# Attention scores from one fp32r product over 96 stacked rows, in an attention and expert kernel on one core

## The chip, the cores and the metric

The kernel runs on one core of a Trainium2 chip. The metric is the device time of one execution in microseconds (us), smaller is better. The core's engines are named as the profile names them: PE (TensorE) and its weight loads PEld, DVE (VectorE), ACT (ScalarE), POOL (GpSimd) and SP (SyncE, which here only issues DMAs).

## The reference, cut to what matters

Two layers run one after the other over x (8 batches x 256 tokens x 256). The change touches only the first mixing step of layer 0, which has 8 heads of 32 dimensions, so 64 pairs of batch and head. q is the layer norm of x, and k and v are both the context:

```python
gate_in = concat([q, k, v], -1)
ig = (gate_in @ igate_w.T + igate_b).T ; fg = (gate_in @ fgate_w.T + fgate_b).T
log_f_cum = cumsum(log_sigmoid(fg))
log_D = where(lower_triangle, log_f_cum[s] - log_f_cum[t] + ig[t], -inf)
max_log_D = max(log_D, over t)
D = exp(log_D - max_log_D)
C = (qh @ kh.T / sqrt(32)) * D
normalizer = maximum(abs(sum(C)), exp(-max_log_D))
h = (C / (normalizer + 1e-6)) @ vh
h_norm = (h - mean(h)) / sqrt(var(h) + 1e-5) * norm_w      # per head
```

After it come a 32-expert layer (top 4), a long convolution with two small feed-forward blocks, and a dense mixture of 8 experts. None of their instructions is changed.

## The kernel before, in words

Semaphores are written by hand, and each engine runs its own list in order.

**Front.** PE transposes the context (L1726, `mix_turned`), two batches and one half of the 256 features at a time, into a PSUM bank, and ACT copies each bank to kT (`mix_copy`, L1215): eight banks. Then PE computes the gates' share of k (`gates`, L1732, started by a wait for all eight copies), and after that the same for q: xn (the normalised rows, DVE L515) is transposed, copied to qT by ACT, and multiplied by the gate weights. `gates_done` releases a chain of small row operations on ACT and DVE (rg, r1, rF, rM, AE, MHL, L520 to L533), which ends with `rows_done`, a transpose by PE (L1759), and aT and eE (L1234, L1235). MHL holds for each of the 64 pairs the negated maximum in two fp32r parts, the high part in rows 0 to 63 and the low part in rows 64 to 127. `sel` (DVE L504) is a table of 64 stationary matrices that pick one pair's two rows out of MHL. `spare` (L1719) issues products whose result nobody reads.

**Scores.** In the loop over i, the 64 pairs, PE runs `scores(i)` and then `values(i - 2)`. `scores` multiplies kT by a masked copy of q in full fp32 over 128 rows, of which 96 are zero: POOL copies the 32 rows of one head into a zeroed slot of qM (`mask_queries`, L1583, 12 slots). The 384 score columns of a head are 256 for the first half of the keys and 128 for the second. Each fp32 product shows as two MATMUL records. The second half of `scores` forms the exponent's argument in another bank: the mask in bf16 over 384 columns (L1777) and the selected maxima in two products of 256 and 128 columns (L1778, L1779).

**Per pair.** ACT exponentiates in two pieces (L1271, L1272), DVE multiplies scores by decay (`mixed`, L603), and PE multiplies the result by v extended by a column of ones (L1788 to L1790, 33 columns each, three products of two passes). Score banks, argument banks and Dm are double, Cm is triple: `scores(i)` waits until DVE has mixed pair i - 2.

**Per batch.** For each finished group of eight pairs DVE does `head_work` in four parts, spread over the next group's pairs: part 0 the normaliser (L562 to L567), part 1 the scaled heads hN (L577), part 2 the mean (L581, L582), and part 3, after ACT has squared (`square`, L1244), the variance (L586, L587). POOL subtracts the mean (`centre`, L1607) and finishes (`finish`, L1596 to L1600: a power, two multiplications, an addition into x). The last two batches are finished by DVE after the loop.

**SP's queue** is in order: loads of ident, context, x and bcv; sixteen stores of zeros into slots_in (L416, 768 KB each); the six convolution constants (L421, after gates_done and vext_done); and, after the last pair's values, gi and w0.

What sets the order around the change is this list:

```python
for i in range(B * NH):          # PE
    scores(i)
    if i >= 2:
        values(i - 2)
```

Of the kernel before, what the change touches and what calls it, by code (L numbers as in the profile page):

```python
# [4 lines left out]
F32 = mybir.dt.float32  # L5
# [8 lines left out]
P = 128  # L14
# [6 lines left out]
NF = 192  # L21
FLOW = 64
# [3 lines left out]
EPS = 1e-5  # L26
ARENA = 212800 // 64 * 64
# [23 lines left out]
def build(nc, dram, out_d):  # L51
    ctx = ExitStack()
    with ctx:
# [70 lines left out]
        vext = at("vext", [P, NT, NH, DH + 1])  # L124
        maskT = at("maskT", [P, 384], BF16)
        idb = at("idb", [P, P], BF16)
        gwt = at("gwt", [P, 6, 16])
# [3 lines left out]
        den = at("den", [P, 2, NH])  # L131
# [10 lines left out]
        sel = at("sel", [P, 64, P], F32R, start["dcw"])  # L142
# [4 lines left out]
        qM = at("qM", [P, 12, SEQ], F32, start["wS"])  # L147
# [3 lines left out]
        Cm = at("Cm", [P, 3, 384], F32, end["Dm"])  # L151
        rg = at("rg", [P, 256], F32, start["sc0"])
# [7 lines left out]
        MHL = at("MHL", [P, 256], F32R, end["ones"])  # L160
        id2 = at("id2", [P, 64], F32, end["MHL"])
# [56 lines left out]
        hN = at("hN", [P, 2, 512], F32, start["h1T"])  # L218
        hQ = at("hQ", [P, 2, 512], F32, end["hN"])
# [7 lines left out]
        assert end["Cm"] <= start["tF"] and end["kc"] <= end["tF"] and end["h1T"] <= start["Dm"] and end["id2"] <= end["cw2"]  # L227
        assert end["hC"] <= end["xn"] and end["hQ"] <= start["Dm"] and end["GI"] <= end["vext"] and end["WF"] <= end["eS"]
# [24 lines left out]
        sel_done = sem("sel_done")  # L253
# [12 lines left out]
        q_masked = sem("q_masked")  # L266
# [6 lines left out]
        head_scaled = sem("head_scaled")  # L273
        head_centred = sem("head_centred")
# [3 lines left out]
        last_centred = sem("last_centred")  # L278
# [47 lines left out]
        residual_added = sem("residual_added")  # L326
        xs_d = nc.dram_tensor("slots_in", (TILES * P, D), F32, kind="Internal").ap()
# [55 lines left out]

        def f32(ap):
            return ap.bitcast(F32)
# [13 lines left out]
        def _(sp):  # L399
# [12 lines left out]

            sp.wait_ge(zero_done, 1)
# [4 lines left out]
            sp.wait_ge(gates_done, 1)  # L418
            sp.wait_ge(vext_done, 1)
            for t, n in ((FZ, "fz"), (FW, "fw"), (Win, "win"), (peT, "pet"), (Wp1, "wp1"), (Wp2, "wp2")):  # L420
                sp.dma_start(t[tuple(slice(None) for _ in t.shape)], dram[n]).then_inc(conv_loaded, 16)  # L421
# [28 lines left out]
        def _(dve):  # L450
# [52 lines left out]
            dve.wait_ge(id2_done, 1)  # L503
            dve.tensor_copy(sel[:, :, :], id2[:, :].unsqueeze(2).to_broadcast([P, 64, P])).then_inc(sel_done, 1)  # L504
# [11 lines left out]
            dve.wait_ge(ctx_loaded, 16)  # L516
            dve.tensor_copy(vext[:, :, :, 0:DH], cx[:, :, :].rearrange("p n (h d) -> p n h d", h=NH)).then_inc(vext_done, 1)
# [41 lines left out]
            def head_normaliser(b, o):  # L559

                dve.wait_ge(pv_done, 8 * (b + 1))
                dve.tensor_copy(den[:, :, :], o[:, :, :, DH])  # L562
                link(dve.tensor_tensor(ut[:, 0, :, :], o[:, :, :, DH], constant(4, [P, 2, NH]), ALU.mult))
# [5 lines left out]
            def head_work(b, part):  # L569
# [3 lines left out]
                if part == 0:  # L573
                    head_normaliser(b, o)
# [24 lines left out]
            for i in range(B * NH):  # L599
# [1728 lines left out]
```

## Time and profile before

| | |
|---|---|
| Median of three runs | 1803.17 us (1802.14 to 1806.01) |
| Span of the profiled execution, first to last instruction | 1787.3 us |
| PE busy in the span | 1667.1 us, 93% |
| DVE, ACT, POOL busy | 1207.9 us, 474.6 us, 471.5 us |
| Mean granted TensorE clock | 0.971 of full speed |
| Front, from the start to the first score product | 46.5 us |
| Loop over 64 pairs | 110.9 us |

The page gives the profiled execution by its span. The median of the runs is 15.9 us above it; this lies before the first and behind the last recorded instruction, or is the difference of one run from another. A matmul's recorded duration includes its way through a pipelined array, so durations of neighbours overlap; how much PE time one takes is read from the distance between two starts. In rows of the timeline the first column is the start in us, the second the duration, and "xN" the merged records.

### The profile page before, as it was taken

The page shows a single profiled execution, that of the slowest core. Times are in us where ns is not written, and L with a number is a line of the kernel's source. Part 1 is how long each engine was busy: PE and PEld are TensorE (multiplying, and loading weights), DVE is VectorE, ACT ScalarE, POOL GpSimd, SP SyncE. Part 2 cuts the span into 40 slices and gives each one's busy share as a digit, 9 for nine tenths or more (in the row PEclk, how much of TensorE's full clock was granted, in tenths as well). Part 3 has the DMA queues.
Part 4 walks back from the last instruction along what each step waited for, and adds up shares of the span by engine and source line. Part 5 has one row for each costly group of instructions (what it writes and reads, how often), then busy time and mean ns, then how long its engine had stood idle before and what let it go on. Part 6 is the DMA issues. An engine that isn't in the chain of part 4 may idle for free.

```text
span 1787.3 us, 29133 instructions
## 1 busy us (share of the span) xinstructions
PE 1667.1 (93%) x9784; PEld 1439.4 (81%) x9785; DVE 1207.9 (68%) x2483; ACT 474.6 (27%) x836; POOL 471.5 (26%) x355
## 2 busy tenths in 40 slices
PE   6998987799956898999999999999999999999998
PEld 5997673388854787888888888888888888888887
DVE  6457777556656895666666766766766766766765
ACT  3445322134432464211211211211111111111111
POOL 4274257688426601100100100100100100100100
PEclk9998999899978998999999999999999999999999
DMA  9200022278643200000000000000000000000001
GB/s 368 91 1 30 16 73 96 89 250 272 200 127 119 72 1 19 19 36 18 19 34 18 20 33 18 21 32 18 21 32 18 23 30 18 26 27 18 18 0 48
DMA packets 53827, 106.53 MB, mean 60 GB/s; under 512 B 6528, under 2 KB 37696, under 8 KB 53632
## 3 DMA queue, kind: packets, MB, share of 16 engines
q1 hardware_dynamic: 19920, 63.33, 10.4%
q10 hardware_dynamic: 27696, 25.51, 4.5%
q0 software_dynamic: 6144, 16.79, 2.9%
q8 instruction: 43, 0.70, 0.2%
q14 instruction: 24, 0.20, 0.0%
HBM read 69.96 MB, written 35.65 MB: 59 GB/s over the span
## 4 chain that ended last, share of the span: by engine, by line
PE 80%; DVE 6%; issue 4%; POOL 4%; DMA 4%; ACT 2%; SPq 0%; POOLq 0%; DVEq 0%; another core or an unknown queue 0%; ACTq 0%
PE ps L1921 39%; PE ps L1937 20%; PE ps L2028 4%; DMA slots_in<-xn,idS 2%; POOL slots_in L1648 2%; PE ps L2047 2%; PE ps L1772 2%; PE ps L2103 1%; PE ps L2125 1%; PE ps L2008 1%; DVE x L917 1%; DMA x<-in_x 1%; PE ps L1773 1%; PE ps L1789 1%; PE ps L1790 1%
## 5 line engine op out<-in xcount | busy, mean ns | idle before, releaser
L1921 PE MATMUL ps<-xTH,wH 128*128 128x512 f32 x1024 | 402.5, 393 | 2.1 <-DVE hF L1161 2.1
L1921 PE MATMUL ps<-xTH,wL 128*128 128x512 f32 x1024 | 402.2, 393 | 0.0
L1921 PE MATMUL ps<-xTL,wH 128*128 128x512 f32 x1024 | 398.9, 390 | 0.0
L1309 ACT ACTIVATE sg<-ps 128x512 f32<-128x512 f32 x264 | 157.9, 599 | 885.3 <-PE ps L1921 885.3
L1161 DVE TENSOR_TENSOR hF<-sg,ps 128x512 f32<-128x512 f32 x256 | 175.7, 686 | 302.1 <-ACT sg L1309 302.1
L1620 POOL TENSOR_TENSOR wL<-wS,wH 128x1536 fp32r<-128x1536 f32 x32 | 111.9, 3496 | 959.8 <-ACT wH L1304 959.8
L1937 PE MATMUL ps<-wL,hH 128*128 128x256 f32 x1024 | 289.8, 283 | 0.0
L1937 PE MATMUL ps<-wH,hL 128*128 128x256 f32 x1024 | 289.7, 283 | 0.0
L1937 PE MATMUL ps<-wH,hH 128*128 128x256 f32 x1024 | 288.6, 282 | 0.5 <-DVE hL L1170 0.5
L1170 DVE TENSOR_TENSOR hL<-hF,hH 128x512 fp32r<-128x512 f32 x256 | 258.0, 1008 | 0.1
L1921 PEld LDWEIGHTS ps<-xTL,wH 128*128 128x128 f32 x1024 | 192.8, 188 | 42.2
L1180 DVE SCALAR_TENSOR_TENSOR x<-ps,cw,x 128x256 f32<-128x256 f32 x512 | 222.6, 476 | 1.0 <-PE ps L1937 1.0
L1921 PEld LDWEIGHTS ps<-xTH,wH 128*128 128x128 f32 x1024 | 193.6, 189 | 36.1 <-ACT sg L1309 1.9
L1921 PEld LDWEIGHTS ps<-xTH,wL 128*128 128x128 f32 x1024 | 193.8, 189 | 30.5
L1937 PEld LDWEIGHTS ps<-wH,hH 128*128 128x128 f32 x1024 | 195.5, 191 | 10.6 <-DVE hL L1170 0.7
L1937 PEld LDWEIGHTS ps<-wH,hL 128*128 128x128 f32 x1024 | 195.5, 191 | 9.8
L1937 PEld LDWEIGHTS ps<-wL,hH 128*128 128x128 f32 x1024 | 195.5, 191 | 0.0
L1164 DVE CAST hH<-hF 128x512 fp32r<-128x512 f32 x256 | 109.3, 427 | 38.8 <-PE ps L1937 30.2
L1648 POOL DMA_INDIRECT slots_in<-xn,idS x64 | 76.6, 1197 | 59.6 <-DMA slots_in<-xn,idS 29.7
L2028 PE MATMUL ps<-eHL,hH 128*128 x384 | 81.5, 295 | 2.2 <-POOL eHL L1635 2.2
L1687 POOL DMA_INDIRECT yg<-slots_out,idG x48 | 50.0, 1041 | 69.2 <-DMA slots_out<-yo 49.0
L603 DVE SCALAR_TENSOR_TENSOR Cm<-ps,Dm 128x384 f32<-128x384 f32 x64 | 35.6, 557 | 47.1 <-ACT Dm L1272 43.0
(385 smaller groups left out, 2525.4 us busy)
## 6 DMA issues: line engine op xcount, KB each, us to landing
wS<-in_w SPq DMA_DIRECT2D x32, 768.0 KB, 4.3
slots_in<-eS SPq DMA_DIRECT2D x16, 768.0 KB, 20.2
eS<-in_wr SPq DMA_DIRECT2D x32, 384.0 KB, 3.9
xl<-slots_in ACTq DMA_DIRECT2D x48, 256.0 KB, 3.9
slots_out<-yo ACTq DMA_DIRECT2D x48, 256.0 KB, 3.1
cx<-in_ctx SPq DMA_DIRECT2D x1, 2048.0 KB, 10.4
x<-in_x SPq DMA_DIRECT2D x2, 1024.0 KB, 13.8
out<-x SPq DMA_DIRECT2D x4, 512.0 KB, 2.9
```

The source lines that it names most:

```text
L1161: dve.tensor_tensor(hF[:, b, :], sg[:, b, :], ps[:, 2 + b, :], ALU.mult).then_inc(mul_done, 1)
L1164: dve.tensor_copy(hH[:, b, :], hF[:, b, :]).then_inc(h_high, 1)
L1170: dve.tensor_tensor(hL[:, b, :], hF[:, b, :], f32(hH[:, b, :]), ALU.subtract).then_inc(h_low, 1)
L1180: dve.scalar_tensor_tensor(x[:, tile, :], acc, cw2[:, tile, bass.ds(it, 1)], x[:, tile, :], ALU.mult, ALU.add).then_inc(evac_done, 1)
L1309: act.activation(sg[:, b, :], ps[:, b, :], ACT.Silu).then_inc(silu_done, 1)
L1620: pool.tensor_tensor(blocks(wL, slot, plain), blocks(wS, slot, plain), f32(blocks(wH, slot, plain)), ALU.subtract).then_inc(w_low, 1)
L1648: pool.indirect_dma_start(xs_d, bass.IndirectOffsetOnAxis(ap=idS[:, n, k:k + 1], axis=0), xn[:, n, :], None, bounds_check=TILES * P - 1, o ...
L1687: pool.indirect_dma_start(slot_rows(n)[:, k, :], None, ys_d, bass.IndirectOffsetOnAxis(ap=idG[:, n, k:k + 1], axis=0), bounds_check=TILES ...
L1772: pe.matmul(ps[:, i % 2, 0:256], kT[:, c, t0:t0 + P], qM[:, i % 12, :], start=True, stop=True)
L1921: last = pe.matmul(ps[:, 2 * half + b, :], piece(w, s, slot, col, P), v[:, k, g * 512:(g + 1) * 512], start=q == 0, stop=q == 5)
L1937: last = pe.matmul(o, h[:, b, t * P:(t + 1) * P], piece(w, s, slot, col, D), start=(opens and t % 2 == 0 and q == 0), stop=(closes and q = ...
L2028: last = pe.matmul(ps[:, 2 + b, t * D:(t + 1) * D], h[:, b, (2 * t + k) * P:(2 * t + k + 1) * P], eFlat[:, bass.ds(off + (w + k * D), D)], ...
```

## The change

The scores come from one fp32r product over 96 rows instead of a full fp32 one over 128. k and q are split into a high part (fp32r) and a low part. `parts` holds them in the transposed layout. They are stored to memory, and for each group of four heads loaded back so that 96 partitions hold, for k, the rows high, low, high, and for q the rows high, high, low of one head (`load_stack`). One product over those 96 rows gives the three leading terms. Four stacks are in the kernel at a time, sixteen are used.

- ACT copies each transposed k bank twice, once as fp32r high part and once as kT. DVE makes the high parts of q. POOL makes all low parts (16 subtractions of 128x512). The masked copies of q, qM and their memset go.
- SP stores the parts (16 DMAs, 8.4 MB in all), loads the stacks (96 DMAs of 128 KB, 12.6 MB), and issues the zero stores between the later stack loads, one per stack.
- The 128-column piece comes first in the banks, so the mask product covers 256 columns and the selector is one product over 384 columns; MHL gains a copy of its second half. The selector is a column of id2 read with step 0; `sel` and its 7.70 us cast go.
- v gets a second extra column, the mean of v over the head, so the mean comes out of the values product (34 columns). `head_work` has three parts; `centre` goes; the normaliser is no longer divided out but enters the variance as eps times its square.
- The constants FZ to Wp2 are issued before the zero stores, not after.

```diff
+            def store_parts(to, g, signal):
+                for i in range(2):
+                    sp.dma_start(to[i, :, :, g * 512:(g + 1) * 512], f32(parts[:, i, :, g * 512:(g + 1) * 512])).then_inc(signal, 16)
+            def load_stack(j):
+                b, c = j // 2, j % 2
+                if j >= STACKS:
+                    sp.wait_ge(qk_done, 4 * (j - STACKS + 1))
+                sp.wait_ge(k_stored[b // 2], 32)
+                sp.wait_ge(q_stored[b // 2], 32)
+                for a, (of, order) in enumerate(((kp_d, (0, 1, 0)), (qp_d, (0, 0, 1)))):
+                    for r, i in enumerate(order):
+                        src = of[i, :, c, b * SEQ:(b + 1) * SEQ].rearrange("(h d) t -> d h t", d=DH)
+                        sp.dma_start(f32(stack(j)[r * DH:(r + 1) * DH, a, :, :]), src).then_inc(stack_loaded[j % STACKS], 16)
+            for g in range(4):
+                sp.wait_ge(k_low, 2 * g + 2)
+                store_parts(kp_d, g, k_stored[g])
+            for g in range(4):
+                sp.wait_ge(q_low, 2 * g + 2)
+                store_parts(qp_d, g, q_stored[g])
+                if g == 0:
+                    load_stack(0)
+            sp.wait_ge(gates_done, 1)
+            for j in range(1, STACKS):
+                load_stack(j)
...
             for a in range(TILES * D // UW):
+                if STACKS + a < 2 * B:
+                    load_stack(STACKS + a)
                 sp.dma_start(zv[a], eS[:, 0:2, :].rearrange("p i c -> p (i c)")).then_inc(zeros_stored, 16)
...
-            dve.wait_ge(id2_done, 1)
-            dve.tensor_copy(sel[:, :, :], id2[:, :].unsqueeze(2).to_broadcast([P, 64, P])).then_inc(sel_done, 1)
...
+            for g in range(4):
+                last = dve.tensor_reduce(vext[:, 4 * g:4 * g + 4, :, DH + 1], vext[:, 4 * g:4 * g + 4, :, 0:DH], AXX, ALU.add)
+                if g == 3:
+                    link(last)
+                    dve.tensor_scalar(vext[:, :, :, DH + 1], vext[:, :, :, DH + 1], 1.0 / DH, None, ALU.mult).then_inc(vext_done, 1)
+                dve.wait_ge(k_stored[g], 32)
+                for c in range(2):
+                    cols_ = slice(g * 512, (g + 1) * 512)
+                    dve.wait_ge(mixT_copied, 8 + 2 * g + c + 1)
+                    dve.tensor_copy(parts[:, 0, c, cols_], qT[:, c, cols_]).then_inc(q_high, 1)
...
-            link(dve.tensor_copy(MHL[0:64, :], r1[0:64, :]))
-            link(dve.tensor_tensor(r2[0:64, :], r1[0:64, :], f32(MHL[0:64, :]), ALU.subtract))
-            dve.tensor_copy(MHL[64:, :], r2[0:64, :]).then_inc(rows_done, 1)
+            link(dve.tensor_copy(MHL[0:64, P:], r1[0:64, :]))
+            link(dve.tensor_tensor(r2[0:64, :], r1[0:64, :], f32(MHL[0:64, P:]), ALU.subtract))
+            dve.tensor_copy(MHL[0:64, 0:P], r1[0:64, P:])
+            dve.tensor_copy(MHL[64:, 0:P], r2[0:64, P:])
+            dve.tensor_copy(MHL[64:, P:], r2[0:64, :]).then_inc(rows_done, 1)
...
                 if part == 0:
-                    head_normaliser(b, o)
+                    dve.wait_ge(pv_done, 8 * (b + 1))
+                    link(dve.tensor_copy(den2[:, :, :, :], o[:, :, :, DH:DH + 2]))
+                    dve.tensor_tensor(hC[:, b, :].rearrange("p (s h d) -> p s h d", s=2, h=NH), o[:, :, :, 0:DH],
+                                      den2[:, :, :, 1].unsqueeze(3).to_broadcast([P, 2, NH, DH]), ALU.subtract).then_inc(head_read, 1)
                 if part == 1:
+                    link(dve.scalar_tensor_tensor(den, den, -1.0, den, ALU.mult, ALU.max))
+                    link(dve.tensor_tensor(den, den, eE[:, :, 8 * b:8 * b + 8], ALU.max))
+                    link(dve.tensor_scalar(den, den, 1e-6, DEN_MAX, ALU.add, ALU.min))
+                    link(dve.scalar_tensor_tensor(mean[:, b % 2, :, :], den, EPS, den, ALU.mult, ALU.mult))
...
-                if i >= 8 and i % 8 in (2, 3, 4):
+                if i >= 8 and i % 8 in (2, 3):
                     head_work(b - 1, i % 8 - 2)
                 if i >= 16 and i % 8 == 1:
-                    head_work(b - 2, 3)
+                    head_work(b - 2, 2)
...
             for j in range(8):
+                act.wait_ge(mixT_done, j + 1)
+                act.activation(parts[:, 0, j % 2, (j // 2) * 512:(j // 2 + 1) * 512], ps[:, j % 4, :], ACT.Identity)
                 mix_copy(j, kT[:, j % 2, (j // 2) * 512:(j // 2 + 1) * 512])
...
-            link(pool.memset(qM[:, :, :], 0.0))
+                    pool.tensor_tensor(parts[:, 1, c, cols_], src[:, c, cols_], f32(parts[:, 0, c, cols_]), ALU.subtract).then_inc(signal, 1)
+            low_parts(kT, 0, k_low)
+            low_parts(qT, 8, q_low)
...
             def scores(i):
-                pe.wait_ge(q_masked, i + 1)
-                pe.matmul(ps[:, i % 2, 0:256], kT[:, c, t0:t0 + P], qM[:, i % 12, :], start=True, stop=True)
-                pe.matmul(ps[:, i % 2, 256:384], kT[:, c, t0 + P:t0 + SEQ], qM[:, i % 12, P:],
-                          start=True, stop=True).then_inc(qk_done, 1)
+                j = i // 4
+                k, q = (stack(j)[0:3 * DH, a, i % 4, :] for a in range(2))
+                wait(pe, mixed_done, i - 1)
+                if i % 4 == 0:
+                    pe.wait_ge(stack_loaded[j % STACKS], 96 * (j // STACKS + 1))
+                pe.matmul(ps[:, i % 2, P:384], k[:, 0:P], q, start=True, stop=True)
+                pe.matmul(ps[:, i % 2, 0:P], k[:, P:], q[:, P:], start=True, stop=True).then_inc(qk_done, 1)
                 wait(pe, decay_done, i - 1)
-                pe.matmul(ps[:, 2 + i % 2, 0:384], idb[:, :], maskT[:, :], start=True, stop=False, skip_group_check=True)
-                pe.matmul(ps[:, 2 + i % 2, 0:256], sel[:, i, :], MHL[:, :], start=False, stop=False, skip_group_check=True)
-                pe.matmul(ps[:, 2 + i % 2, 256:384], sel[:, i, :], MHL[:, P:SEQ], start=False, stop=True,
+                pe.matmul(ps[:, 2 + i % 2, 0:256], idb[:, :], maskT[:, 0:256], start=True, stop=False, skip_group_check=True)
+                pe.matmul(ps[:, 2 + i % 2, 0:384], id2[:, i:i + 1].to_broadcast([P, P]), MHL[:, :], start=False, stop=True,
                           skip_group_check=True).then_inc(arg_done, 1)
```

## Rows read from the trace of the kernel before

**Rows 1.** Busy time by stretch: span part, busy us and records per engine, clock, DMA
```profile
0.00:46.50 46.50, 31.77 (x176) 25.68 (x177) 31.19 (x87) 15.12 (x27) 20.09 (x39) 1.00 0.99 370
46.50:157.40 110.90, 110.20 (x833) 105.87 (x833) 62.27 (x162) 50.53 (x135) 64.47 (x81) 1.00 0.09 31
```

**Rows 2.** Waits from 46 to 157 us: total us, times, longest
```profile
ACT Dm L1271 <- PE ps L1779: 59.1, 64, 1.6
DVE Cm L603 <- ACT Dm L1272: 43.0, 50, 1.5
```

**Rows 3.** Timeline, one pair of the loop, from score product to score product
```profile
80.18 0.68 PE L1772 MATMUL ps<-qM,kT 128*128 128x256 f32 x2
...
80.69 0.38 PE L1773 MATMUL ps<-qM,kT 128*128 128x128 f32 x2
...
80.91 0.33 PE L1777 MATMUL ps<-maskT,idb 128*128 128x384 bf16 x1
...
81.25 0.36 PE L1788 MATMUL ps<-vext,Cm 128*128 128x33 f32 x2
...
81.45 0.47 ACT L1271 ACTIVATE Dm<-ps,aT 128x256 f32<-128x256 f32 x1 [0.98 <-PE ps L1779]
...
81.83 0.36 ACT L1272 ACTIVATE Dm<-ps,aT 128x128 f32<-128x128 f32 x1
...
81.89 0.68 PE L1772 MATMUL ps<-qM,kT 128*128 128x256 f32 x2
...
82.27 0.56 DVE L603 SCALAR_TENSOR_TENSOR Cm<-ps,Dm 128x384 f32<-128x384 f32 x1 [0.45 <-issue]
```

**Rows 4.** Timeline, PE in the last stage, fp32r products of 256 and 512 columns
```profile
800.18 0.28 PE L1937 MATMUL ps<-wL,hH 128*128 128x256 f32 x1
800.30 0.40 PE L1921 MATMUL ps<-xTH,wH 128*128 128x512 f32 x1
800.53 0.40 PE L1921 MATMUL ps<-xTH,wL 128*128 128x512 f32 x1
```

**Rows 5.** Timeline, DVE in the loop, a mix and the head work behind it
```profile
65.14 0.56 DVE L603 SCALAR_TENSOR_TENSOR Cm<-ps,Dm 128x384 f32<-128x384 f32 x1 [1.16 <-ACT Dm L1272]
65.61 0.17 DVE L562 COPY den<-ps 128x16 f32<-128x16 f32 x1
...
66.10 0.17 DVE L565 TENSOR_TENSOR den<-den,eE 128x16 f32<-128x16 f32 x1
66.31 0.18 DVE L566 TENSOR_TENSOR den<-den,kc 128x16 f32<-128x16 f32 x1
...
67.44 0.68 DVE L577 TENSOR_TENSOR hN<-ps,den 128x512 f32<-128x512 f32 x1
```

**Rows 6.** Timeline, the front: copies of k, its gates, the last row cast
```profile
12.90 0.60 ACT L1215 ACTIVATE kT<-ps 128x512 f32<-128x512 f32 x1 [4.13 <-PE ps L1726]
...
16.31 2.07 ACT L1215 ACTIVATE kT<-ps 128x512 f32<-128x512 f32 x4 [0.25 <-PE ps L1726]
...
18.52 7.15 PE L1732 MATMUL ps<-kT,gateW 128*128 128x256 f32 x32 [0.88 <-ACT kT L1215]
...
44.99 0.29 DVE L533 CAST MHL<-r 64x256 fp32r<-64x256 f32 x1
```

**Rows 7.** Timeline, POOL and DVE just after the loop
```profile
157.55 1.26 POOL L1599 TENSOR_TENSOR hC<-hC,bcv 128x512 f32<-128x512 f32 x1
157.74 1.10 DVE L564 TENSOR_TENSOR den<-den,ut 128x16 f32<-128x16 f32 x1
```

**Rows 8.** Timeline, SP's DMA issues
```profile
11.86 19.25 SPq L416 DMA_DIRECT2D slots_in<-eS  x16
...
37.59 0.46 SPq L421 DMA_DIRECT2D FW<-in_fw  x1
```

**Rows 9.** Busy time by stretch, columns as in rows 1, around the loop's end
```profile
155.00:158.00 3.00, 2.84 (x22) 2.44 (x21) 1.99 (x6) 0.73 (x2) 2.84 (x3) 1.00 0.00 0
158.00:161.00 3.00, 3.00 (x7) 0.62 (x5) 2.86 (x5) 0.00 (x0) 2.10 (x2) 0.77 0.86 314
```

More of the change, by code:

```diff
@@ L21 @@
 NF = 192
+STACKS = 4
 FLOW = 64
@@ L26 @@
 EPS = 1e-5
+DEN_MAX = 1e15
 ARENA = 212800 // 64 * 64
@@ L140, in build @@
         assert top[0] - base <= ARENA, top[0] - base
-        sel = at("sel", [P, 64, P], F32R, start["dcw"])
+        parts = at("parts", [P, 2, 2, NT * P], F32R, start["dcw"])
+        stackA = at("stackA", [P, 2, 2, 4, SEQ], F32R, start["wS"])
+        stackB = at("stackB", [P, 2, 2, 4, SEQ], F32R, start["xTH"])
         qT = at("qT", [P, 2, NT * P], F32, start["xTH"])
@@ L151, in build @@
         Cm = at("Cm", [P, 3, 384], F32, end["Dm"])
+        gwt = at("gwt", [P, 6, 16], F32, start["Cm"])
         rg = at("rg", [P, 256], F32, start["sc0"])
@@ L159, in build @@
         ones = at("ones", [P, 256], F32, end["AE"])
-        MHL = at("MHL", [P, 256], F32R, end["ones"])
-        id2 = at("id2", [P, 64], F32, end["MHL"])
+        MHL = at("MHL", [P, 384], F32R, end["ones"])
+        id2 = at("id2", [P, 64], F32R, end["MHL"])
         hC = at("hC", [P, B, 512], F32, start["xn"])
@@ L217, in build @@
         wf = at("wf", [P, 4, D], F32, start["vext"])
-        hN = at("hN", [P, 2, 512], F32, start["h1T"])
-        hQ = at("hQ", [P, 2, 512], F32, end["hN"])
+        hQ = at("hQ", [P, 2, 512], F32, start["h1T"] + 4096)
         WF = at("WF", [P, 8, D], F32, start["eS"])
@@ L227, in build @@
         assert end["Cm"] <= start["tF"] and end["kc"] <= end["tF"] and end["h1T"] <= start["Dm"] and end["id2"] <= end["cw2"]
+        assert end["parts"] <= end["ya"] and end["stackA"] <= start["FW"] and end["stackB"] <= end["xTH"]
         assert end["hC"] <= end["xn"] and end["hQ"] <= start["Dm"] and end["GI"] <= end["vext"] and end["WF"] <= end["eS"]
@@ L265, in build @@
         rowsT_copied = sem("rowsT_copied")
-        q_masked = sem("q_masked")
+        k_low = sem("k_low")
+        q_high = sem("q_high")
+        q_low = sem("q_low")
+        k_stored = [sem(f"k{g}_stored") for g in range(4)]
+        q_stored = [sem(f"q{g}_stored") for g in range(4)]
+        stack_loaded = [sem(f"stack{i}_loaded") for i in range(STACKS)]
         qk_done = sem("qk_done")
@@ L382, in pairs_done, with stack @@
             return 0 if isinstance(k, int) and k <= 0 else k * 2 + 1
+        def stack(j):
+            return (stackA, stackB)[j % STACKS // 2][:, j % 2, :, :, :]
         def f32(ap):
@@ L410, in load @@
                 sp.dma_start(blocks(wS, slot, plain), src.rearrange("p (a c) -> p a c", c=BLK)).then_inc(stage_loaded[slot], 16)
+            def store_parts(to, g, signal):
[22 more added lines that the diff above has]
+                load_stack(j)
+            sp.wait_ge(vext_done, 1)
+            for t, n in ((FZ, "fz"), (FW, "fw"), (Win, "win"), (peT, "pet"), (Wp1, "wp1"), (Wp2, "wp2")):
+                sp.dma_start(t[tuple(slice(None) for _ in t.shape)], dram[n]).then_inc(conv_loaded, 16)
             sp.wait_ge(zero_done, 1)
@@ L1238, in square @@
             def square(b):
-                if b < B - 1:
-                    act.wait_ge(head_centred, b + 1)
-                else:
-                    act.wait_ge(last_centred, 1)
+                act.wait_ge(head_read, b + 1)
                 wait(act, head_var, b - 1)
@@ L2262, in constants @@
     mask = np.zeros((P, 3 * P))
-    mask[:, 0:P] = mask[:, 2 * P:] = np.where(t <= s, 0.0, -1e30)
+    mask[:, 0:P] = mask[:, P:2 * P] = np.where(t <= s, 0.0, -1e30)
     tri = np.stack([(t < s) * 1.0, np.ones((P, P))], 1)
```

99 lines of the change are left out of this document (27 added, 72 removed).

## The prediction

> **What bounds the kernel now.** I read the busy time by stretch first, because the change touches two stretches only. The front lasts 46.5 us and the loop over 64 pairs 110.9 us [rows 1]; everything behind keeps its instructions. In the loop PE is busy for 110.20 of 110.90 us at full granted clock, DVE and ACT for about half. The waits agree: ACT waits for PE's argument product before each of the 64 pairs, 59.1 us in all, and DVE waits for ACT, 43.0 us [rows 2]. So PE paces the loop, and what counts is the distance between its starts.
>
> One pair's row of starts [rows 3]: score products 80.18 and 80.69, mask 80.91, values 81.25, next pair 81.89. So a pair costs 1.71 us: 0.51 + 0.22 for the scores, 0.34 for mask and selectors (384 + 256 + 128 columns), 0.64 for values. 64 x 1.71 = 109.6, and 1.3 us of start and end make up the 110.9.
>
> **The change, part by part.**
>
> *Scores.* Two fp32r products of 256 and 128 columns. An fp32r product of 256 columns takes 0.12 us to the next start, one of 512 takes 0.23 [rows 4], so time goes with columns. I take 0.12 for the first. The second is not in the trace in this form: half of it is 0.06, and a values product's six passes in 0.64 [rows 3] say that about 0.11 goes to each new stationary block, however few columns follow. I take 0.09, bounds 0.06 and 0.12. That 96 rows are used instead of 128 I cost at nothing. Saved: 0.73 - 0.21 = 0.52 a pair.
>
> *Mask and selector.* 640 columns instead of 768: 0.34 x 640/768 = 0.28, saves 0.06. *Values* with 34 columns instead of 33: 0.64 as before. PE's pair becomes 0.12 + 0.09 + 0.28 + 0.64 = 1.13 us.
>
> *Does something else bind at 1.13?* The chain over two pairs: `scores(i)` waits for the mix of pair i - 2. Today from the first score product to ACT's start is 1.27 us, from there to DVE's mix 0.82, the mix 0.56 [rows 3]; with 0.04 for PE's restart and 0.58 less in front the ring is 0.69 + 0.82 + 0.56 + 0.04 = 2.11 for two pairs, 1.06 each. That is only 0.07 below PE. Today's slack of 0.37 a pair is gone, so what DVE does between mixes now shows.
>
> *DVE's head work.* A mix holds DVE for 0.47 until the next operation starts; a small linked operation costs 0.21, one over 512 elements 0.68 [rows 5]. The new part 0 is a copy and a subtraction, 0.91; part 1 four small ones, 0.84; part 2 a reduction and a small one, 0.93. Each sits behind the mix of pair 2, 3 or 1 of eight, so these three take 3 x 0.47 + 2.68 = 4.09 us against PE's 3.39: 0.70 late in eight pairs, and with nearly no slack PE doesn't win it back. ACT's square (0.5) lands on two exponentials of 0.38 each [rows 3]: 1.26 against 1.13, 0.15 late. Eight pairs: 9.04 + 0.85 = 9.9, or 1.24 a pair. Loop: 64 x 1.24 + 1.3 = 80.7, **30.2 us less**. Bounds: PE alone, 64 x 1.13 + 1.3 = 73.6 (37.3 less); head work costing its whole 2.68 + 0.5 in each eight, 0.12 for the short product and some port waits, about 1.45 a pair and 94 (17 less).
>
> *Feeding the stacks.* PE's only new wait is for `stack_loaded` before each fourth pair; all PE work queues behind it. An issue on SP costs 0.46 (FW [rows 8]). Stack 0 is stored and loaded once the first q parts exist, around 34 us; stacks 1 to 3 follow gates_done, 18 issues of 0.46, 8.3 us from about 42, before pair 4 is due. In the loop four pairs (5.0 us) need seven issues, 3.2 us, and 1.57 MB (a stack and a zero store); at the 370 GB/s of the front [rows 1] that is 4.2 us, asked for 12 pairs ahead. So the loop's transfers are hidden, by 0.8 us in 5. The zero stores are read long after the loop; their old 19.25 us of issue [rows 8] overlapped the front. The six constants are issued ahead of them, needed only at 157. All at nothing.
>
> *The front.* ACT now copies each k bank twice. Four copies take 2.07, 0.52 each; the first starts at 12.90 and the last ended at 18.38, and PE's gates of k started at 18.52 on that release [rows 6]. Sixteen copies end at 12.9 + 16 x 0.52 = 21.2: 2.8 us later. Behind `gates(kT)` are PE's transposes of q, its gates and so gates_done, in order, so the 2.8 passes through to rows_done. Two more casts of half length before rows_done, against 0.29 for a full one [rows 6]: +0.5. The `sel` cast ran while DVE waited for x: nothing back. DVE's four reductions of v and eight casts of q, and POOL's subtractions, lie beside PE's work on q: the same number of gate products as for k, 7.15 [rows 6], and the transposes, some 10 us together.
>
> *A port.* A 16-column DVE operation on SBUF takes 0.17 alone [rows 5] but 1.10 when a POOL subtraction or product over 512 is under way, and ends with it [rows 7]. The front gets 16 such POOL operations beside DVE's small root steps and q casts. I take 0.5 for the delay, bounds 0 and 2 (two stalls of 1.1). The Trainium skill, "SBUF — State Buffer", on the shared port pair, says that a DVE instruction with two SBUF inputs and a GpSimd one that reads SBUF exclude each other for the whole instruction. By that rule POOL's eight q subtractions and DVE's eight q casts would run strictly in turn, 8 x 1.26 and 8 x 0.4, 13 us (an estimate) beside PE's 10, and the sum would be some 2 us higher, 1779; the trace agrees on the small operation, and nothing in it shows a cast being held.
>
> Front: 2.8 + 0.5 + 0.5 = **3.8 us more**, bounds 2.8 and 6. A gain I see only in x arriving with fewer stores beside it, some tenths.
>
> *Behind the loop.* DVE loses a reduction and a subtraction, but PE goes on with products of its own until ACT is freed, so 0.
>
> **Sum.** -30.2 + 3.8 = -26.4. It is made against the profiled span of 1787.3 us: 1760.9. The median lies 15.9 above the span, and I keep that distance: 1803.2 - 26.4 = **1776.8 us**.
>
> **The rivals.**
>
> 1. *The clock falls in the loop (slower).* At 158 to 161 us the granted clock drops from 1.00 to 0.77 as a mean, which is its two levels 2.4 and 1.2 GHz mixed, although PE's records look full; ahead of it PE ran the last values products, short ones, at 155 to 158 [rows 9]. The new loop has a larger share of those: 0.64 of 1.24 us instead of 0.64 of 1.71, with gaps. At 1.2 GHz a pair would cost 2 x 1.13 = 2.26, the whole loop 146, and the sum +35.1 + 3.8: 1842. It decides from (26.4 / (2.26 - 1.24)) = 26 pairs at the low level on; with fewer it only eats the gain, near 1792 with 15. Against it: the loop before holds 1.00 throughout, its last three us included [rows 1, 9]. The Trainium skill, "TensorE: Matmul & The Clock Gate", Part 1, says that the throttled state is the default and activity releases it; taken alone it would allow this case and gives no reason to rule it out. 0.06 for the full case, 0.08 for the partial one.
>
> 2. *The stacks arrive late.* The rows have 1 KB runs and three partition groups of 32; the trace shows no such transfer. At 250 GB/s instead of 370, 1.57 MB take 6.3 us, 1.57 a pair for the last 48 pairs: 48 x 0.33 = 16 more, 1793. For it: the cover is 0.8 us in 5. Against: twelve pairs of lead. 0.08.
>
> 3. *The score product doesn't get cheaper,* because an fp32r product on stacked rows runs at the pace of the full fp32 one. Then a pair stays at 1.65, the loop at 107, and the gain of 4 is what the front costs: 1803. Rows 4 speak against it. 0.04.
>
> **How the numbers follow.** The forecast, loop at 1.13 to 1.4 a pair, has 0.72, the rivals 0.26, and 0.02 stays for a front that costs over 25 us. Within the forecast the low end is 1803.2 - 37.3 + 2.8 = 1768.7 and the high one 1803.2 - 17 + 6 = 1792. A DVE whose part lateness is absorbed, with x early, could give 3 us more, so I set 1766; the top goes to 1794 to hold the late stacks. Outside are the two slow cases, rival 3 and part of rival 1. About 0.2%, 3.6 us, is what a measurement of this kernel can tell from no change. Faster: 0.72 + 0.08 + 0.08 = 0.88; same 0.04; slower 0.08.
>
> **What the profile would show.** Right: the distance between a pair's first score starts at 1.13 in the pairs without head work and over 1.3 in pairs 1 to 3 of eight; the score products 0.12 and 0.09 apart; DVE above 70% busy in the loop; `gates(kT)` starting at about 21.3 and the loop at about 50.3; no wait of PE on DMA in the loop; clock 1.00 in it. Wrong: PE waiting for the stack loads, a clock under 1.00 inside the loop, SP's issues nearer 1 us than 0.46, or the loop starting after 53.

## The result, and the profile after

The changed kernel takes 1849.15 us (median of four runs, 1842.77 to 1854.84) against 1804.59 for the kernel before beside it (1802.14 to 1809.28): 1.0242 times as long, interval 1.0207 to 1.0278, 44.6 us more. It is slower, where 26 us less was forecast. Executions of one kernel can differ in where the clock falls: where some held it and some did not, the experiments below list the times, or give the ratio of those that held it and name the other.

The page's clock line of the changed kernel, one digit for each fortieth of the span:

```profile
PEclk9555699879996799899999999999999999999999
```

Between about 46 and 185 us the granted clock is near half. Busy time by stretch (span part, busy us and records of PE, PEld, DVE, ACT, POOL, clock, DMA share, GB/s) shows the fall:

```profile
0.00:53.00 53.00, 34.67 (x175) 28.29 (x176) 37.26 (x101) 18.48 (x35) 29.99 (x42) 0.92 0.80 272
53.50:191.20 137.70, 136.79 (x642) 136.46 (x641) 64.40 (x140) 50.41 (x135) 39.36 (x24) 0.51 0.62 196
...
47.00:52.00 5.00, 2.36 (x15) 1.26 (x13) 4.24 (x12) 1.90 (x3) 0.00 (x0) 0.96 1.04 392
52.00:55.00 3.00, 3.00 (x14) 2.44 (x13) 2.25 (x9) 0.68 (x3) 0.00 (x0) 0.51 0.97 304
55.00:58.00 3.00, 2.09 (x17) 1.84 (x17) 1.25 (x3) 1.86 (x6) 0.00 (x0) 1.00 0.98 251
58.00:62.00 4.00, 4.00 (x21) 3.99 (x20) 1.54 (x3) 1.47 (x4) 0.00 (x0) 0.55 1.13 253
62.00:190.00 128.00, 128.00 (x595) 128.00 (x594) 60.70 (x131) 46.86 (x125) 39.36 (x24) 0.50 0.60 194
```

The first two rows answer to [rows 1]: a loop of 137.7 us where there were 110.9, at a clock of 0.51 where there was 1.00. The others narrow it down. After five microseconds in which PE was busy for 2.36 the clock is at its lower level, 1.2 GHz (0.51); it comes back for three (1.00), falls once more at about 58, two microseconds after a wait of 0.91 us that is shown below and with PE full in between, and stays at 0.50 for 128 us, in every one of which PE has a record. A full PE in the records is thus no sign of a high clock. The profiled runs of e2, e4 and e8 below come back in their first pairs as well; what sets this one apart from e2 and e8 is the second fall.

PE's timeline, the starts of two pairs in a row at the high level, then a whole pair and the start of the next at the low one (the bracket is the idle time ahead and what ended it):

```profile
56.24 0.39 PE L1794 MATMUL ps<-stackA 96*128 96x256 f32 x1 [0.91 <-DVE Cm L644]
...
57.42 0.36 PE L1794 MATMUL ps<-stackA 96*128 96x256 f32 x1
...
104.20 0.56 PE L1794 MATMUL ps<-stackB 96*128 96x256 f32 x1
104.56 0.31 PE L1795 MATMUL ps<-stackB 96*128 96x128 f32 x1
104.67 0.44 PE L1798 MATMUL ps<-maskT,idb 128*128 128x256 bf16 x1
...
105.23 0.47 PE L1808 MATMUL ps<-vext,Cm 128*128 128x34 f32 x2
...
106.36 0.56 PE L1794 MATMUL ps<-stackB 96*128 96x256 f32 x1
```

From first score product to first score product: 1.18 us at 56 us, near the forecast 1.13; 2.16 at 104. The pair before the change took 1.71 [rows 3], at the high level throughout. The waits (us in total, times, longest) from 53 to 192 us keep the shape of [rows 2], with no wait of PE on a DMA among them. PE's only wait there is 0.9 us for DVE's first mix, so no late stack dropped the clock in this execution:

```profile
ACT Dm L1305 <- PE ps L1799: 84.9, 63, 1.8
DVE Cm L644 <- ACT Dm L1306: 67.4, 54, 1.6
```

**Where the time is.** Between the two profiled executions the first score product moves from 46.5 to 53.3 (+6.8), the loop grows from 110.8 to 137.8 (+27.0), and from the loop's end to the first scatter (POOL's first indirect store, at 213.3 and 255.3) it is 64.2 instead of 56.0 (+8.1). Together 41.9, near the 44.6 between the medians. The two profiled spans differ by more, 65.6 us; the other 23.7 lie between the first scatter and the last stage, where no instruction is changed. That part takes 503.7 us before and 527.3 in the changed kernel, but 503.9 in e1 below and 523.4 in e13, so it goes up and down from execution to execution and these 23.7 are not put down to the change.

The front, timelines of four engines:

```profile
51.82 0.69 PE L1782 MATMUL ps<-ident,AE 128*128 128x128 f32 x2 [2.64 <-DVE MHL L583]
...
33.73 11.66 POOL L1617 TENSOR_TENSOR parts<-qT,parts 128x512 fp32r<-128x512 f32 x8 [9.03 <-DVE parts L565]
...
39.95 2.90 DVE L565 CAST parts<-qT 128x512 fp32r<-128x512 f32 x2
42.89 1.37 DVE L568 SCALAR_TENSOR_TENSOR r<-rg 64x256 f32<-64x256 f32 x1
...
41.40 1.30 SPq L438 DMA_DIRECT2D stackA<-k_parts  x3
...
44.16 6.29 SPq L426 DMA_DIRECT2D q_parts<-parts  x6
50.56 3.00 SPq L438 DMA_DIRECT2D stackA<-k_parts  x3
```

PE stands idle for 2.64 us ahead of the last transposes before the loop, waiting for DVE's last row operation. DVE's last two casts of q take 2.90 us beside POOL's subtractions, and the root step behind them (L568; the same operation took 0.42 before) takes 1.37. SP asks for stack 0 only at 41.4 and for stack 1 at 50.6.

### The profile page after: what moved, and what is told of

Its sections match the earlier page's. It is cut to its first block, busy times and chain, and to the rows that moved or that the text cites. A ratio compares the mean times of both kernels' runs of the same rounds, so it can differ in the third digit from the quotient of the medians.

```text
span 1852.9 us, 28721 instructions
## 1 busy us (share of the span) xinstructions
PE 1713.6 (92%) x9592; PEld 1481.3 (80%) x9593; DVE 1215.6 (66%) x2472; ACT 477.7 (26%) x844; POOL 454.3 (25%) x299
## 4 chain that ended last, share of the span: by engine, by line
PE 79%; DVE 5%; issue 4%; POOL 4%; DMA 4%; ACT 2%; another core or an unknown queue 1%; POOLq 0%; DVEq 0%; SPq 0%; ACTq 0%
PE ps L1941 38%; PE ps L1957 20%; PE ps L2048 4%; DMA slots_in<-xn,idS 3%; PE ps L2067 2%; POOL slots_in L1671 2%; PE ps L1810 1%; PE ps L1809 1%; PE ps L1794 1%; PE ps L2145 1%; PE ps L2123 1%; PE ps L2028 1%; PE ps L1799 1%; PE ps L1808 1%
```

## The experiments

Two theories stood. One: the new pair is as short as forecast, but too light to hold the high level past a stall of PE or to climb back from the low one, and stalls come at the loop's entry or behind a late stack. The other: the score product on 96 stacked rows, or the stream of stack loads, is what costs or what holds the clock down, whatever PE did before. "High" and "low" below are 2.4 and 1.2 GHz.

**More work for PE in each pair.** J stands for this unread product, put ahead of the mask product; here and below the code is shortened:

```
+ pe.matmul(ps[:, 2 + i % 2, 0:384], idb[:, :], maskT[:, :], start=True, stop=True, skip_group_check=True)   # J
  e1: J in each pair    e8: J twice in each pair    e3: J if i < 8
  e2: k, q = (f32(stack(j)[0:3 * DH, a, i % 4, :]) for a in range(2))
  e4: mask product over maskT[:, :], 384 columns
```

> The changed kernel with one more bf16 product of 384 columns in each pair, written into the argument bank ahead of the mask product, which overwrites it. Theory A (the loop's own array work is too light to hold the 2.4 GHz level, so it falls and stays at 1.2): the granted clock stays 1.00 in the loop, a pair costs 1.13 + 0.16 = about 1.3 us, the loop about 86 us instead of 137.7, the time 1785 to 1795. Theory B (the stack loads or the 96-row products are slow by themselves): the pair stays above 2.1 us or grows, 1850 to 1860.

> The changed kernel with the score products over the same 96 stacked rows in full fp32, that is with the array work of the kernel before. Theory A: clock 1.00 in the loop, a pair near 1.7 us as before, loop 110 us, time 1808 to 1815 (before plus what the front costs). Theory B: a pair of 2.1 us plus the 0.5 us that full fp32 costs, 2.6 us, 1880.

> The extra product in the first 8 pairs only. Theory A (the steady loop cannot hold the level): the clock falls a few us after pair 8, loop 8 x 1.3 + 56 x 2.16 = 131 us, time 1840 to 1848. Theory A2 (the level is lost only through the stalls at the loop's entry, and a pair at 2.4 GHz would keep it): clock 1.00 to the end of the loop, pairs of 1.2 us, loop 80 us, time about 1782.

> The changed kernel with the mask product 384 columns wide as before (the added 128 columns are zero): 0.05 us more array work per pair. Theory A: if this little is enough, clock 1.00 and a pair of 1.2 to 1.25 us, time about 1785; if it is not, the loop stays at 1.2 GHz with pairs of 2.27 us and the time is 1850 to 1858. Theory A2: as the changed kernel, 1850 to 1858, since the entry is the same.

> Two extra 384-column products per pair, the entry as in the changed kernel. Theory (at the low level the share of work per pair decides whether the loop climbs back): with two, the level recovers within some us after the entry in most runs, pairs about 1.45 us, loop 95 us, time about 1788 where before takes 1792. Rival (once low, always low): pairs 2.16 + 0.64 = 2.8 us, loop 180 us, about 1875.

Measured: e1 1847.81, 1838.29, 1860.50 and 1778.96, beside 1792.5 before. e2 1.0043 (1.0014 to 1.0073) from three runs, and a fourth at 1890.03. e3 1.0212 (1.0175 to 1.0248). e4 1.0239 (1.0193 to 1.0286). e8 0.9976 (0.9952 to 1.0000), ten runs from 1795.80 to 1805.61. The stretches of e2, then of e8:

```profile
53.00:57.00 4.00, 4.00 (x15) 3.19 (x14) 2.23 (x8) 0.82 (x4) 0.00 (x0) 0.57 0.97 265
57.00:150.00 93.00, 93.00 (x694) 89.33 (x694) 48.88 (x124) 45.76 (x123) 33.55 (x21) 1.00 0.89 281
```

```profile
52.00:55.00 3.00, 3.00 (x16) 2.20 (x14) 1.63 (x6) 0.58 (x3) 0.00 (x0) 0.58 0.98 259
55.00:62.00 7.00, 6.24 (x51) 5.47 (x49) 2.78 (x5) 3.65 (x11) 0.00 (x0) 1.00 1.10 244
62.00:149.00 87.00, 86.79 (x709) 79.15 (x708) 50.95 (x130) 46.48 (x125) 39.04 (x24) 1.00 0.88 284
```

Both enter the loop low (0.57, 0.58), as the changed kernel does, and both are high from 57 or 55 us to the end, with the same stack loads beside them. So neither the 96 rows nor the stack traffic holds the clock down. But climbing back at the entry is not what distinguishes them: the changed kernel does it at about 55 us as well, and so does e4. They differ in that no second fall follows. No trace has the loop of e2 or e8 at the low level behind its entry, so whether their heavier pairs could lift it from there isn't shown. Adding two products to every pair makes the kernel 2.6% faster (e8's 0.9976 against 1.0242, from two batches): its loop is 96.8 us with them, 137.8 without. e2 answers rival 3 as well: fp32 on the same stacks is 105.3 us of loop, so the cheaper product is real. Its fourth run is 92 us slower, about what its loop of 105.3 would lose at the low level throughout (an estimate with the factor 2.16 / 1.15 between the pairs of this kernel at the two levels); it has no trace, but it speaks against a pair of this weight always climbing back. One J does not lift the level: e1's profiled execution fell at 51 us and stayed low to 225, with J in every pair of its loop:

```profile
52.00:213.00 161.00, 160.45 (x709) 148.73 (x710) 67.80 (x147) 51.01 (x137) 39.13 (x24) 0.50 0.55 172
```

Its one good run (1778.96) shows what the time could be. e3 was low at 51 us too, and its eight pairs with J did not lift it; whether they would have held the high level it does not tell. e4 was high at 55 to 75 and then lost it:

```profile
72.87 0.39 PE L1810 MATMUL ps<-vext,Cm 128*128 128x34 f32 x2
77.28 0.55 PE L1794 MATMUL ps<-stackA 96*128 96x256 f32 x1 [4.02 <-DMA stackA<-q_parts]
```

In this timeline of PE it waited 4.02 us for a stack, and the product after it is at the low pace (0.55 for 256 columns, 0.36 at the high one). The clock fell at 75.3, two microseconds into the wait. The forecast had costed those loads at nothing.

**The entry.** Here PE's filling products in front of `rows_done` and behind k's gates grow, with the aim of no gap before the loop.

```
- spare(6, 42)
+ spare(6, 58)                                            # e5, e6, e7; e6 and e7 with J in each pair
+ if j >= 3: 4 x pe.transpose(ps[:, 6, ...], cx[:, t, 0:P], ident[:, :])   # e7: unread, in the phase of k
```

> The changed kernel with 58 instead of 42 unread products before rows_done, so that PE isn't idle for 2.64 us ahead of the loop; nothing added in the loop. If only the entry loses the level: clock 1.00 through the loop, pairs 1.2 us, time below before by 1 to 1.5%, some 1770 on the chip where before takes 1792. If the steady loop can't hold it: the level falls somewhere in the loop and stays down, 1820 to 1840, as in the run with the 384-column mask, which fell at 75 us.

> 58 unread products at the entry and one extra 384-column product per pair. Theory (two things are needed: enter at the high level and do enough work per pair to keep it; once low the loop can't climb back): every run, not one of four, is at the level of the one good run before, 1775 to 1782, loop about 85 us. Rival (the level is lost at random in the loop even so): some runs at 1820 to 1860.

> The same, and four unread transposes behind each of the last five context banks in the front, where the changed kernel ran its k gates at 1.2 GHz (10.06 us instead of 7.15). If that fall comes from PE waiting for ACT's doubled copies: the gates of k take 7.2 us again and the time is 2 to 4 us below the run with entry and loop products alone. If it is not: no difference.

Measured: e5 1.0175 (1.0133 to 1.0218); e6 1844.54, 1846.43, 1843.62 and 1786.04; e7 1.0260 (1.0204 to 1.0315). PE's timeline in e5, then in e6, then DVE's in e7:

```profile
57.31 0.39 PE L1810 MATMUL ps<-vext,Cm 128*128 128x34 f32 x2
58.89 0.55 PE L1794 MATMUL ps<-stackA 96*128 96x256 f32 x1 [1.19 <-DMA stackA<-q_parts]
```

```profile
77.45 0.36 PE L1794 MATMUL ps<-stackA 96*128 96x256 f32 x1 [2.86 <-DMA stackA<-q_parts]
```

```profile
36.93 0.75 DVE L565 CAST parts<-qT 128x512 fp32r<-128x512 f32 x2
...
40.10 2.91 DVE L565 CAST parts<-qT 128x512 fp32r<-128x512 f32 x2
```

With the entry filled the clock fell later in e5 and e6, and close to a wait for a stack: 0.7 us into the wait of pair 4 in e5 (1.19 us), and 1.2 us after the end of pair 16's wait in e6 (2.86), whose first product still has the high pace. In e5 a wait of 1.10 us for the first mix lies 3.2 us ahead of the fall, so e5 does not separate the two. In e7 the filling did not reach: PE was idle for 2.93 us ahead of the last transposes, the clock was at 0.50 from 51.3 us and its whole loop stayed there. e7 had k's gates in 7.14 us instead of 10.06, yet its loop still began at 53.5: k's gates alone were not what the loop waited for. It waited for DVE, whose last two casts of q took 2.91 us where the two before took 0.75. POOL subtracts beside both; in these two the casts took 1.5 us each, against 0.41.

**Feeding the stacks.** e9 moves q's high parts from DVE to ACT, asks for stack 0 after the second store, and spreads the remaining traffic (the wait for the last zero store moves from DVE, behind the loop, to a later place on ACT):

```
  ACT: + activation(parts[:, 0, j % 2, ...], ps[:, j % 4, :], ACT.Identity).then_inc(q_high, 1)   # DVE's casts of q go
  SP:  - load_stack(0) after store g == 0, six constants, then a zero store behind each stack
       + load_stack(0) after store g == 1
       + behind each further stack one zero store or one constant in turn; ten zero stores behind the loop
  PE:  - spare(6, 42)
       + spare(6, 50)
```

e10 is e9 with J, e11 with J twice, e12 is e10 with e7's transposes.

> The changed kernel fed earlier: ACT, not DVE, makes the high parts of q; stack 0 is loaded after the second store of q; the six constants and six of the sixteen zero stores go one by one between the stack loads, the other ten zero stores after the loop; 50 unread products at the entry. Nothing is added in the loop. Theory F (the falls in the three kernels before came from PE waiting 1.2 to 4.0 us for a stack; the steady loop holds 2.4 GHz by itself): no wait of PE on a stack, clock 1.00 in the loop, pairs 1.2 us, loop 79 us, time 1.5 to 2% below before. Theory S (the steady loop is too light): the level falls in the loop with no wait ahead of it, time 1.5 to 2.5% above before. For the front: POOL's eight subtractions for q, 11.66 us beside DVE's casts, should take 9 to 9.9 us, and the loop start 1 to 3 us earlier than at 53.3.

> The same with one extra 384-column product per pair. Theory F: no wait on stacks, all runs high, pairs 1.3 us, about 6 us over the fed kernel alone, 1 to 1.5% below before, where without the feeding three of four runs fell. Theory S allows this too if one product is enough; falls in some runs with no wait ahead of them would speak for S and against one product.

> The same with two extra products. High in all runs under either theory, pairs 1.45 us, loop 95 us; 3 to 5 us better than two products without the feeding (0.9976 of before) if the front gets shorter, so a ratio near 0.995.

> One extra product per pair, fed, and unread transposes in the k phase so that the gates of k run at 2.4 GHz. With DVE's casts of q gone, the 2.9 us that PE wins there should now reach the loop's start (with the casts in place they did not: 53.5 against 52.9 us). 2 to 3 us below the fed kernel with one product.

Measured, against the kernel before in each batch: e9 0.9862 (0.9831 to 0.9892) from four runs of 1766.31 to 1770.55, and a fifth at 1835.30; e10 0.9893 (0.9856 to 0.9930), e11 0.9958 (0.9936 to 0.9980), e12 0.9889 (0.9851 to 0.9927), no low run in these three. Loops: 85.9, 96.0 and 85.9 us for e10 to e12. One J with late stacks (e1, e6, e7) was low in ten of twelve runs, with punctual ones (e10, e12) in none of eight; but in the traces of e1 and e7 the fall came at an unfilled entry, and only e6 ties it to a stack. The fifth run of e9 is the one that was profiled, PE's timeline and the stretch behind it:

```profile
54.19 0.39 PE L1795 MATMUL ps<-stackA 96*128 96x256 f32 x1 [1.09 <-DVE Cm L642]
...
55.00:60.00 5.00, 5.00 (x30) 5.00 (x30) 1.67 (x3) 2.18 (x6) 0.00 (x0) 0.63 1.12 236
```

No wait for a DMA is in it: the clock fell at 56 us, behind the 1.09 us in which the third pair waits for the first mix. So the loop's own start can do it too, and needs some cover. It is also the place of the changed kernel's own second fall, behind the wait of 0.91 us. Where one J or more filled part of this start, waits of 0.92 (e10), 0.93 (e6, e12), 0.77 (e11) and 0.76 (e8) were passed at the high level.

**The two causes apart.** e13 is e9 with J twice in pairs 0 to 3 only, `spare(6, 53)` and e7's transposes. e14 has this same cover, but the change's own feeding of the stacks and its own casts of q (with `spare(6, 75)`, so that PE is filled up to its later start):

```
+ for _ in range(2 if i < 4 else 0): J
```

> The fed kernel with the entry covered: 53 unread products, two extra 384-column products in each of pairs 0 to 3 only, unread transposes in the k phase. Nothing from pair 4 on. Theory F (the loop holds 2.4 GHz by itself once it is entered there and never waits for a stack): all runs high, pairs 1.2 us, time 1.4 to 1.8% below before, 3 to 6 us better than with one product in each pair. Theory S (the steady loop is too light, and four good runs of five were luck): falls in some runs, 3% more in those.

> The same cover of the entry (75 unread products, since rows_done comes later here; two products in pairs 0 to 3; transposes in the k phase) on the changed kernel's own feeding. Theory F: PE waits for a stack, 1 us or more at pair 4 or 3 to 4 us at pair 16, the level falls right behind that wait and stays down, 1.5 to 2.5% above before. If the entry alone was at fault: all runs high and the time within 5 us of the fed kernel.

Measured in one batch, before at 1807.13: e13 0.9887 (0.9866 to 0.9907), 1784.80, six runs from 1783.14 to 1790.83; e14 1.0147 (1.0123 to 1.0171), 1833.28, four runs from 1830.77 to 1835.30. The stretches of e13, then of e14:

```profile
60.00:70.00 10.00, 10.00 (x88) 9.92 (x87) 5.89 (x16) 6.44 (x18) 0.00 (x0) 1.00 1.10 277
...
52.40:131.60 79.20, 78.13 (x650) 76.22 (x649) 54.53 (x141) 49.77 (x135) 39.03 (x24) 1.00 0.91 234
```

```profile
65.00:70.00 5.00, 5.00 (x46) 5.00 (x44) 3.60 (x11) 2.93 (x8) 0.00 (x0) 1.00 1.05 347
70.00:75.00 5.00, 3.03 (x26) 2.84 (x25) 2.16 (x4) 2.62 (x7) 0.00 (x0) 0.83 1.10 256
75.00:80.00 5.00, 3.73 (x18) 3.76 (x18) 0.56 (x1) 1.05 (x3) 0.00 (x0) 0.50 1.08 326
80.00:85.00 5.00, 5.00 (x25) 5.00 (x24) 2.85 (x7) 1.88 (x6) 2.94 (x1) 0.50 1.07 328
```

And the stall in e14, SP's issues of that stack, PE's two products around the wait, and two short stretches at its start:

```profile
60.98 0.43 SPq L454 DMA_DIRECT2D FZ<-in_fz  x1
...
64.40 1.27 SPq L438 DMA_DIRECT2D stackA<-k_parts  x3
65.72 1.38 SPq L438 DMA_DIRECT2D stackA<-q_parts  x3
...
72.64 0.39 PE L1815 MATMUL ps<-vext,Cm 128*128 128x34 f32 x2
76.27 0.55 PE L1797 MATMUL ps<-stackA 96*128 96x256 f32 x1 [3.23 <-DMA stackA<-q_parts]
...
73.00:73.30 0.30, 0.03 (x1) 0.00 (x0) 0.00 (x0) 0.21 (x1) 0.00 (x0) 1.00 1.07 249
73.50:74.00 0.50, 0.00 (x0) 0.00 (x0) 0.36 (x1) 0.00 (x0) 0.00 (x0) 0.50 1.14 227
```

The stack of pair 16 is issued at 64.4 to 67.1, behind six constants, and lands at about 76: nine microseconds in a DMA that is full (share 1.05 to 1.10). PE waits for 3.23, the clock goes from 1.00 to 0.50 and stays there, so that e14's loop takes 130.4 us. It falls when PE has been idle for 0.3 to 0.5 us, so the trace ties the fall to this place, not to the length of the wait; that all four runs of e14 are slow and none of e13's six is what speaks for the late stack. e13, whose loop begins at the same time (52.35, e14's at 52.21) with the same work in it, holds 1.00 to the end in 79.2. The medians are 48.5 apart. What in e9's feeding did it (constants, zero stores, the earlier stores of q) was not tried one by one, and e13 and e14 differ also in who makes q's high parts and in the number of filling products.

Plain pairs of the loop at the high level, e13, PE's timeline:

```profile
103.25 0.36 PE L1798 MATMUL ps<-stackB 96*128 96x256 f32 x1
103.45 0.22 PE L1799 MATMUL ps<-stackB 96*128 96x128 f32 x1
103.51 0.28 PE L1804 MATMUL ps<-maskT,idb 128*128 128x256 bf16 x1
103.81 0.31 PE L1814 MATMUL ps<-vext,Cm 128*128 128x34 f32 x2
...
104.40 0.37 PE L1798 MATMUL ps<-stackB 96*128 96x256 f32 x1
```

## Why the prediction was wrong

**The scores, the pair and DVE's lateness: right, at the high level.** A plain pair is 1.15 us, forecast 1.13. Its terms: scores 0.20 + 0.06 = 0.26 (forecast 0.12 + 0.09), mask and selector 0.30 (0.28), values 0.59 (0.64). The first score product was too cheap: the row it was taken from ran behind another product, here it follows the values (that this is the reason was not tried). Pairs with head work take up to 1.29 (105.59 to 106.88 in e13; over 1.3 was named), the loop 79.2 (forecast 80.7), DVE is busy for 54.53 of it, 69% (over 70% named). The 30 us of the loop are there.

**Rival 1 is what happened, at 0.06 chance.** Its price was near: 2.16 us a pair (2.26), a median of 1849 (1842). That the sum comes so close is partly luck: the loop grew by 27.0, not 35.1, while the front and the part behind the loop grew by 14.9, not 3.8. The steps that failed are its two reasons. It took the shorter values products as the only danger and the loop before, at 1.00 throughout [rows 1], as evidence against. But that loop's pair has 0.73 us of fp32 score products, the very work the change takes out; with it back (e2) three of four runs were at before's level, and with two unread products (e8) all ten, where the changed kernel was slow in four of four. The loop before said nothing of a lighter pair, nor of how such a pair stands a gap: the light pair stays at the level it is at, 128 us at 0.50 in the changed kernel and 79.2 at 1.00 in e13. And the gaps that decide it were costed at nothing: PE's 2.64 us ahead of the last transposes and 0.91 for the first mix, behind which the changed kernel's profiled execution fell for good. The second failed reason is that the rival stood apart from rival 2: the late stack was priced at its own length. In that execution PE waits for no stack, as forecast, but once the start is covered it does: e13 against e14 shows 3.23 us of waiting and 51 us of loop.

The Trainium skill, "TensorE: Matmul & The Clock Gate", Part 1, on the default state, was named there as the rule that leaves this open. The runs agree with it as far as the low level returns behind idle stretches (in the changed kernel PE is idle for 2.64 us, and the clock is at 0.50 from 52 us) and is left while PE works (e2, e8). They add that PE's records at 128 of 128 us did not release it. Why the light pair falls at 58 us and the pairs of e2 and e8 don't, and whether two J could lift the level within the loop, stays open here.

**Feeding the stacks at nothing: wrong in three terms.** The 370 GB/s came from the front's plain streams [rows 1]; at a DMA share of 1.0 to 1.1 the loop's mix moved 244 to 347. The constants were counted as issues only; their bytes (2.3 MB) stand ahead of pair 16's stack, and it came 2.9 to 4.0 us late in e4, e6 and e14. Stack 1 was to be issued from about 42; SP issued it at 50.6, because it waits in order, first for stores of q to land (36.9 to 41.4) and then issues six more in 6.29 us, 1.05 each: for the stores the forecast's own sign, nearer 1 us than 0.46, came true, for the stack loads (0.43 each) it didn't. Pair 4 then waits 1.19 in e5; in the changed kernel, already slower, it doesn't.

**The front: +6.8 instead of +3.8.** The copies did what was said: the last of k's ends at 21.6 (21.2 forecast). Not forecast was that PE, idle for 3.15 us while it waits for them, then runs most of k's gates at the low level (0.50 from 21 to 27.5 us): 10.06 us instead of 7.15. The claim that a delay there passes straight to `rows_done` failed: e7 moves the end of k's gates three us forward and nothing follows. The loop began at 53.3, past the 53 that was named as a sign of being wrong. What set the start in e7 was DVE, behind its casts of q, and in both the root step at 1.37. The forecast took 0.5 for the port and noted that no row showed a cast being held; here two of the eight are slow beside POOL, at 1.5 us each, while six pass at 0.41 and POOL pays instead (its eight subtractions take 11.66, where 8 x 1.26 [rows 7] make 10.1). The Trainium skill, "SBUF — State Buffer", on the shared port pair, names casts in a two-port mode too among what can shut GpSimd out and be shut out; the rule as the forecast gave it, for two SBUF inputs, would not cover a cast, which has one. The trace agrees on the root step, which has two (1.37), and in part on the casts, but not on strict turns: POOL and DVE were through with q 12.2 us after the first cast began, where the forecast drew 13. For the front the sum that the forecast drew from that page, 5.8 us, was nearer to 6.8 than its 3.8; since k's gates are in the 6.8 too, it doesn't confirm that term.

**Behind the loop at nothing: wrong, +8.1,** and not by the level the loop left alone: e4 and e14 leave their loops low too and take 56.3 and 56.6 us to the first scatter, like before (56.0). In the changed kernel the clock was back at 1.00 by 202 us, fell again at 208.6 within the second of two waits of PE for ACT (1.87 and 3.04 us; before has 1.57 and 3.04), and stayed low for 17 us, with PE full from the end of that wait on:

```profile
203.20:207.20 4.00, 2.07 (x14) 1.41 (x14) 3.59 (x13) 3.98 (x8) 0.00 (x0) 1.00 0.01 4
211.20:223.20 12.00, 12.00 (x26) 6.59 (x24) 6.06 (x28) 6.01 (x13) 0.00 (x0) 0.50 0.00 0
```

Before falls within the same wait, at 173.3, and is high again at 176.7, after 3.4 us. e5 has the changed kernel's course (64.1), e9 a longer low stretch there (64.1 too). What decides between the courses was not tried.

**The distance of 15.9 us between span and median was misread.** Each run's own span is about 1.9 below its time (1852.9 and 1854.84; 1.8 to 3.4 over all runs), so the profiled execution of before took about 1789 and was simply a quick one; medians of before range from 1792 to 1807 over the batches. That is no reason for the miss, but a forecast of a difference should be set against the median only.

**What the forecast is worth with the clock held:** e13 is 22.3 us below before in its batch (1784.80 against 1807.13), forecast 26.4. Its loop is 31.6 shorter, its loop begins 5.9 later (52.35 against 46.5), and 3.4 are in neither stretch (this sets two profiled executions against medians). In the two traces the first scatter comes 24.0 us earlier, at 189.3 against 213.3.

## What to carry to other kernels

Before taking work out of TensorE, ask what the lighter loop would do behind a gap of one to a few microseconds, at its start above all, not only in steady state; a loop that never left the high level is no evidence for a lighter one. Price a possible wait of TensorE by what it can trigger, and where a change moves operands through memory, count every byte queued on the rings ahead of the first late consumer and every landing for which the issuing queue waits in order. If a level must be held, a few unread products at the entry together with punctual loads (e13) cost less loop time than two products in each pair (e8, 96.8 us against 79.2). One in each pair with punctual loads and the same transposes (e12) was as good over the whole kernel, 0.9889 against 0.9887 (two batches).

## What the runs showed of the hardware that was not expected

- Unread work can pay: two more 384-column products in each pair made the changed kernel's loop 96.8 us instead of 137.8, by the clock alone (0.50 and 1.00).
- The low level can last with PE's records unbroken: 128 us at 0.50 in the changed kernel.
- The last idle time of PE around a fall was 0.91 us (the changed kernel), 1.09 (e9), 1.19 (e5), 2.86 (e6), 3.23 (e14) and 4.02 (e4), but the fall did not wait for its end: it came 0.3 us into it in e14, 0.7 in e5 and 2.0 in e4, and 1.2 to 2.1 us after it in e6, e9 and the changed kernel. e13 had 0.76, e10 0.92 and e12 0.93 at the same place of the start and held, and by their times four runs of e9 held as well.
- Behind the loop, around the same wait of 3.04 us, the low level lasted 17 us in the changed kernel and 3.4 before, with the same instructions.
- Going from the high level to the low one made a pair 1.88 times as long (2.16 against 1.15).
- The sixteen DMA engines at a share above 1.0 moved 244 GB/s in one stretch (e8, 55 to 62 us) and 392 in another (the changed kernel, 47 to 52).
